# Audio tower on one core: second norm, routing and scatter of the first mixture moved into the recurrence, group by group

## What is computed

```python
h = tok(x, weight, bias)
h = h + lru(layernorm(h))              # complex diagonal recurrence over 166 steps, 256 states
h = h + moe16(layernorm(h))            # first mixture, below
h = h + sparse_attention(layernorm(h))
h = h + moe64(layernorm(h))            # dense over 64 experts, top 42
...
# first mixture
gate_logits = x @ gate_weight.T
top_vals, top_idx = jax.lax.top_k(gate_logits, TOP_K)     # 2 of 16
routing_w = jax.nn.softmax(top_vals, axis=-1)
h = jax.nn.silu(jnp.einsum('td,efd->tef', x, w1))
h_sum = jnp.einsum('tef,te->ef', h, mask)                  # per expert, over its tokens
h_mean = h_sum / jnp.maximum(counts, 1)[:, None]
y_mean = jnp.einsum('ef,edf->ed', h_mean, w2)
out = jnp.einsum('tk,tkd->td', routing_w, y_mean[top_idx])
```

## Time and profile before

| | us |
|---|---|
| median of 3 runs (2101.24 to 2106.53) | 2101.55 |
| span of the profiled execution | 2100.1 |
| profiled execution around its span, by the median | 1.45 |
| PE, DVE, ACT, POOL busy | 1869.5, 1683.1, 1385.2, 1349.0 |
| tokens, first norm, tables | 0 to 101.9 |
| recurrence, groups 0 to 3 | 101.9 to 188.4 |
| second norm and token product | 188.4 to 225.3 |
| routing on DVE | 225.3 to 252.4 |
| scatter by POOL (and late weights to 314.5) | 252.4 to 364.5 |
| 43 tiles, then the down product | 369.8 to 478.7 |
| attention, router of the second mixture | 478.7 to 884 |
| second mixture | 884 to 2100 |

### The profile page before, as it was taken

One profiled execution on the slowest core, in us unless ns is written; L12 is line 12 of the kernel. 1 busy time (PEld: TensorE's weight loads), 2 busy tenths in 40 slices (PEclk: granted clock), 3 DMA queues, 4 the chain that ended last, 5 costly groups with the idle time before them and its releaser, 6 DMA issues.

```text
span 2100.1 us, 50357 instructions
## 1 busy us (share of the span) xinstructions
PE 1869.5 (89%) x17138; PEld 1348.3 (64%) x17138; DVE 1683.1 (80%) x4788; ACT 1385.2 (66%) x2075; POOL 1349.0 (64%) x1027
## 2 busy tenths in 40 slices
PE   7889310888998997899999999999999999999998
PEld 5556200455657985677777777777777777777776
DVE  4775830865567859799999999999999999999998
ACT  4112350743444545688888888888888888888886
POOL 2100177007950003498998989899889989888887
PEclk9999655998998995699999999999999999999999
DMA  3613181622310020000000200000200000000000
GB/s 92 182 40 121 52 293 60 124 39 77 109 60 1 1 84 1 1 2 1 0 0 1 81 2 1 0 0 1 82 2 0 0 0 2 2 10 11 10 10 18
DMA packets 73500, 82.65 MB, mean 39 GB/s; under 512 B 38565, under 2 KB 56517, under 8 KB 71685
## 3 DMA queue, kind: packets, MB, share of 16 engines
q1 hardware_dynamic: 70660, 75.19, 12.0%
q0 software_dynamic: 2688, 5.44, 0.8%
HBM read 42.97 MB, written 29.20 MB: 34 GB/s over the span
## 4 chain that ended last, share of the span: by engine, by line
PE 58%; DVE 3%; issue 1%; ACT 1%; POOL 0%; ACTq 0%; DVEq 0%; POOLq 0%
PE bank L2447 29%; PE bank L2430 27%; DVE m_work L2321 1%; PE bank L405 1%; DVE m_best L2318 0%; DVE m_work L2312 0%; PE bank L414 0%; PE bank L2400 0%; DVE m_ut L851 0%; ACT m_h L2253 0%; DVE m_best L2311 0%; DVE m_ex L2323 0%; DVE h L2359 0%; POOL m_h L2198 0%; DVE m_red L2324 0%
## 5 line engine op out<-in xcount | busy, mean ns | idle before, releaser
L2447 PEld LDWEIGHTS bank<-weights,m_h 128*128 128x128 f16 x10752 | 639.3, 98 | 189.1 <-DVE hc L2350 95.2
L2198 POOL TENSOR_TENSOR m_h<-m_hidden,m_h 128x896 f16<-128x896 f32 x384 | 725.2, 1888 | 31.9
L2350 DVE SCALAR_TENSOR_TENSOR hc<-bank,m_shares,hc 128x128 f32<-128x128 f32 x2688 | 726.9, 341 | 4.0 <-PE bank L2447 4.0
L2447 PE MATMUL bank<-weights,m_h 128*128 128x128 f16 x10752 | 724.2, 219 | 2.3 <-POOL m_h L2198 2.3
L2250 ACT ACTIVATE m_hidden<-bank,m_b 128x896 f32<-128x896 f32 x384 | 386.7, 1007 | 183.1 <-PE bank L2430 183.1
L2335 DVE TENSOR_TENSOR m_h<-bank,m_h 128x896 f16<-128x896 f32 x384 | 419.0, 1091 | 101.8 <-ACT m_h L2253 101.8
L2196 POOL TENSOR_SCALAR m_h<-m_hidden 128x896 f16<-128x896 f32 x384 | 359.8, 937 | 104.2 <-ACT m_hidden L2250 78.9
L2430 PE MATMUL bank<-m_u_first,weights 128*128 128x448 f16 (+1 forms) x1536 | 417.9, 354 | 5.5 <-DVE h L2359 5.5
L2430 PE MATMUL bank<-m_u_second,weights 128*128 128x448 f16 (+1 forms) x1536 | 417.6, 354 | 0.0
L2247 ACT ACTIVATE bank<-bank,m_b 128x896 f32<-128x896 f32 x384 | 377.2, 982 | 0.7 <-PE bank L2430 0.7
L2253 ACT ACTIVATE m_h<-bank 128x896 f16<-128x896 f32 x384 | 348.7, 908 | 0.0
(11 more groups left out here) (333 smaller groups left out, 2165.6 us busy)
## 6 DMA issues: line engine op xcount, KB each, us to landing
weights<-expert_factors SPq DMA_DIRECT2D x12, 1024.0 KB, 7.8
expert_slots<-lru_zeros SPq DMA_DIRECT2D x1, 8256.0 KB, 32.0
lw_raw<-e_w_dram SPq DMA_DIRECT2D x16, 512.0 KB
expert_factors<-lw_made SPq DMA_DIRECT2D x16, 512.0 KB
ew_raw<-e_w_dram SPq DMA_DIRECT2D x16, 512.0 KB, 3.9
lru_wst<-w_dram SPq DMA_DIRECT2D x16, 256.0 KB, 2.7
weights<-w_dram SPq DMA_DIRECT2D x1, 4096.0 KB, 12.7
expert_factors<-ew_made SPq DMA_DIRECT2D x8, 512.0 KB, 3.1
```

What stands on the lines that cost most here:

```text
L2198: g.tensor_tensor(h1[:, x, 1], hidden[:, x], h1[:, x, 0], ALU.subtract).then_inc(second_of[1], 1)
L2350: last = v.scalar_tensor_tensor(acc[:, m * TW:(m + 1) * TW], y[q][:, (n - start) * TW:(n - start + 1) * TW], shares[:, m, e:e + 1], acc[:, ...
L2447: last = t.matmul(y[q][:, (n - start) * TW:(n - start + 1) * TW], factors[:, m, n * TW:(n + 1) * TW], k.weights[:, grp % 2, 2 + m, at], st ...
```

## The change

Routing becomes a class, `Routing`, whose parts are called from the recurrence's programs. A group has 11 tiles (`GT`), the last of 48 rows. While group g is in the recurrence, group g-1 is normed, routed and sent. Each expert has a fixed region of `REGION` rows in HBM, so a token's place is its expert's base plus a running count (`start`), and needs no totals of later groups. The rows behind an expert's last are zeroed at the end (`sync_fill`), and tiles are read at rows given by a register. The late weights move from ACT and DVE to POOL, behind the sends; SP stores them, and loads the down weights, between the tiles. The raw product lies where the down weights lay before (`k.weights[:, 1]`).

```diff
+REGION = -(-(T + ST) // ST) * ST
+SPARE = E0 * REGION
+GT = -(-GTOK // TW)
+PASSES = tuple((m, min(m + 3, GT)) for m in range(0, GT, 3))
@@ class Routing
+    def sync_fill(self, sp):
+        sp.wait_ge(self.tables, 1)
+        for e in range(E0):
+            row = sp.value_load(self.fill_i[0:1, e:e + 1], min_val=e * REGION, max_val=e * REGION + T)
+            sp.dma_start(k.slots[bass.ds(row, ST), :]..., blank).then_inc(self.filled, 16)
+    def pool_send(self, pool, r):
+        pool.wait_ge(self.second, r + 1)
+        pool.wait_ge(self.slots, r + 1)
+        for m in range(GT):
+            for q in range(2):
+                g.indirect_dma_start(out=self.k.slots, ...).then_inc(self.sent[r > 0], 16)
+    def pe_products(self, pe, r, b, y_added, u_ready):
+        if b == 0:
+            pe.wait_ge(y_added, STEP * (r + 1))
...
+        for m in range(first, end):
+            last = self.nc.tensor.matmul(out[0:rows_in(m), m - first], self.k.h[:, tokens_of(r, m)], self.cgi[:], ...)
+    def act_raw(self, act, r):
+            sc.activation(self.raw[:, first:end], self.token_bank(r, b), ACT.Copy).then_inc(self.raw_kept, 1)
...
+                last = sc.activation(self.u_tok[...], self.raw[:, m, 0:128], ACT.Square, accum_out=self.sums[:, m:m + 1])
+    def act_rows(self, act, r):
+        sc.activation(self.st[:, 1], self.st[:, 0], ACT.Sqrt).then_inc(self.root, 1)
...
+        for m in range(GT):
+            last = sc.activation(self.u_tok[...], self.raw[:, m, 0:128], ACT.Identity, scale=self.scale[:, m:m + 1])
+        act.wait_ge(self.gaps, r + 1)
+        sc.activation(self.gap[:], self.gap[:], ACT.Exp).then_inc(self.expd, 1)
@@ recurrence, POOL
+                if c == PERG + 1:
+                    routing.pool_start(pool)
+            for r in range(NGR):
+                routing.pool_send(pool, r)
@@ recurrence, ACT
-            for n in range(NC):
-                widen(n)
+            for g in range(NGR):
+                if g:
+                    routing.act_raw(act, g - 1)
+                    routing.act_rows(act, g - 1)
+                for i in range(STEP):
+                    widen(STEP * g + i)
@@ recurrence, DVE
                 if g + 1 < NGR:
                     state_part(g + 1, 0)
+                if g:
+                    routing.dve_scales(dve, g - 1)
+                    routing.dve_choose(dve, g - 1)
+                for i in range(2):
+                    add(g, i)
+                    split(STEP * g + i)
+                    if g == 0:
+                        normed(2 * PERG + 2 * i)
+                        normed(2 * PERG + 2 * i + 1)
+                if g:
+                    routing.dve_place(dve, g - 1)
+                    routing.dve_rows(dve, g - 1)
+                    routing.dve_weights(dve, g - 1)
                 if g + 1 < NGR:
                     state_part(g + 1, 1)
...
+            routing.dve_scales(dve, NGR - 1)
+            routing.dve_choose(dve, NGR - 1)
+            routing.dve_rows(dve, NGR - 1)
+            routing.dve_place(dve, NGR - 1)
+            routing.dve_weights(dve, NGR - 1)
+            routing.dve_tables(dve)
@@ recurrence, PE
+                if g:
+                    for b in range(len(PASSES)):
+                        routing.pe_products(pe, g - 1, b, y_added, u_ready)
                 for i in range(STEP):
+                    if i == 2 and g:
+                        routing.pe_rank(pe, g - 1)
                     output(g, i)
@@ first_mixture, SP
+            W2_AT = (2, 5, 8, 11)
+            KEEP_FROM, KEEP_EVERY = 4, 5
             for j in range(NST):
                 if j >= RING:
                     sp.wait_ge(up, PARTS * (j - RING + 1))
-                sp.dma_start_transpose(xt[:, j % RING], k.slots[j * ST:(j + 1) * ST, :])...
+                row = sp.value_load(row_i[0:1, j:j + 1], min_val=0, max_val=SPARE)
+                sp.dma_start_transpose(xt[:, j % RING], k.slots[bass.ds(row, ST), :])...
+                if j in W2_AT:
+                    sp.dma_start(w2[:, es], a["w2"][:, es]).then_inc(k.w2_in, 16)
+                if j >= KEEP_FROM and (j - KEEP_FROM) % KEEP_EVERY in (0, 2):
+                    late.sync_keep(sp)
@@ LateWeights
+    def sync_keep(self, sp):
+        self.sync_load(sp, i + 2)
+        sp.wait_ge(self.split, i + 1)
+        sp.dma_start(self.k.kept[...], self.made[:, i % 2]).then_inc(self.kept_out[i % 2], 16)
+    def pool_piece(self, pool, i):
+        g.tensor_copy(out[:, 0], raw).then_inc(self.rounded, 1)
+        g.tensor_tensor(left, raw, out[:, 0], ALU.subtract).then_inc(self.raw_read, 1)
+        g.tensor_scalar(left, left, 1.0 / SHARE, 1.0, ALU.mult, ALU.mult).then_inc(self.widened, 1)
+        g.tensor_tensor(out[:, 1], left, out[:, 0], ALU.add).then_inc(self.split, 1)
```

More of the change, by code:

```diff
@@ L531, in recurrence @@
+BIG = float(1 << 20)
+def recurrence(nc, k, tables, routing):
     a = k.a
@@ L552, in recurrence @@
         piece = E0 * FF0 // NC
-        wst = sb("wst", [128, 2, piece])
-        wide = sb("wide", [128, 2, piece])
-        zeros = sb("zeros", [128, 2 * 128], F16)
+        room = k.weights[:, 1].rearrange("p a b -> p (a b)")
+        raw_room, room = room[:, 8 * piece:], room[:, 0:8 * piece].bitcast(F32).rearrange("p (a b c) -> p a b c", a=2, b=2)
+        wst, wide = room[:, 0], room[:, 1]
+        routing.begin(ctx, on_diag[:], tables.work[:], va[:], raw_room)
         diag_ready = sem("diag_ready")
@@ L904, in first_mixture @@
         xt = sb("xt", [128, RING, 2, ST], F16)
[L906 to L911, removed]
+        rt = routing.rt
+        owner_i, row_i, owned = routing.owner_i, routing.row_i, routing.owned
         cleared = sem("outputs_cleared")
[L913 to L917, removed]
-        s = sem("routing_step")
-        expd = sem("exp_ready")
-        counted = sem("counted")
-        ranked = sem("ranked")
-        slots = sem("slots_ready")
-        shared = sem("weights_ready")
-        owners = sem("owners_ready")
-        turned = sem("weights_turned")
-        rt_ready = sem("rt_ready")
-        sent = sem("rows_sent")
         x_in = [sem(f"x_in{p}") for p in range(RING)]
@@ L1076, in _ @@
-            for q in range(2):
-                last = v.tensor_tensor_scan(halves(upto[:])[:, q], going[:].rearrange("p e n -> p (e n)"), totals[:, q], 0.0,
-                                            ALU.mult, ALU.add)
-            link(last)
-            count, whole, ends, start = few[:, 0], few[:, 1], few[:, 2], few[:, 3]
-            v.tensor_tensor(halves(place[:]), halves(upto[:]), totals, ALU.subtract)
-            link(v.tensor_scalar(whole, upto[:, :, NTW - 1], 1.0 / ST, 0.5 - 0.5 / ST, ALU.mult, ALU.add))
@@ L1099, in _ @@
-            link(v.reciprocal(tot[:, 1], tot[:, 0]))
-            v.tensor_tensor(wt[:], gap[:], wide(tot[:, 1]), ALU.mult).then_inc(shared, 1)
-            for i in range(late.count // 2):
-                late.dve_piece(dve, i)
-            link(v.tensor_tensor(past[:], line[:].unsqueeze(2).broadcast_to([128, NST, E0 - 1]),
-                                 ends[:, 0:E0 - 1].unsqueeze(1).broadcast_to([128, NST, E0 - 1]), ALU.is_ge))
-            link(v.tensor_reduce(owner[:], past[:], X, ALU.add))
@@ L1114, in _ @@
-            link(v.tensor_tensor(owned[:, 0], owned[:, 0], few[0:NST, 4], ALU.mult))
-            for i in range(late.count // 2, late.count):
-                late.dve_piece(dve, i)
             for j in range(PARTS * NST):
@@ L1191, in _ @@
                     pe.wait_ge(added, c - 3)
-                t.matmul(k.bank[:, c % 4, 0:CW], ym[:], k.hc[:, span(c)], start=True, stop=True).then_inc(out, 1)
+                t.matmul(k.bank[:, c % 4, 0:size(c)], ym[:], k.hc[:, span(c)], start=True, stop=True).then_inc(out, 1)
 class Choice:
```

640 lines of the change are left out of this document (387 added, 253 removed).

## The result

The changed kernel takes **2065.15 us** (median of 4 runs, 2062.78 to 2067.7), the kernel before 2101.39 beside it: a ratio of 0.9821, with a 95% interval of 0.9807 to 0.9835. The forecast was 2065. The total is right to the microsecond, and that is luck: the four executions alone lie 4.9 us apart, and errors of the working cancel. The experiments are mostly about that working. The profiled execution is the slowest of the four (2067.7); its span is 2065.9 us.

The account below looks back on a forecast made before the run. The path was taken as recurrence, second norm, routing, 112 us of POOL, then tiles. Sends gain 76 us, but slower tiles cut the gain to 37.0: 2100.1 - 37.0 = 2063.1 in the span, 2065 us as median; range 2044 to 2090.

Parts of the forecast that it names:

- Recurrence: Recurrence with norm and routing of each group inside it: ends at about 228 instead of 188.4, 40 us later.
- Sends: 88 sends on POOL beside the recurrence, 1.38 us each, POOL the bound from group 2: end at 288 instead of 364.5.
- the 3 us added for a slower TensorE: Added to the sends' end for TensorE running slower in groups 2 and 3 of the recurrence.
- The block change: Between the sends and the mixture's tiles: takes 1.0 us, so that POOL starts splitting pieces at 293.
- The tiles: First mixture: POOL's 6.6 us a piece holds the tiles, which leave 4.55; end at 410.9 instead of 447.9.
- 103 us of transfers: DMA work beside the tiles: transposes 45, pieces 47, down weights 11, in some 115 us; 4 us taken for it.
- Two signs: In the tiles' stretch: SP waiting for the splits, and POOL splitting without pause from about 293 to 400.
- Rival 1: Tiles are bound by DMA or SP, not POOL: loop ends 10 to 25 later, 2075 to 2090 us; chance 0.17.
- 91 us for SP: SP's need in the tile loop: 43 x (1.21 + 0.64) + 16 x 0.7, binding only if a register load exceeds 1.2.
- Rival 2: TensorE stays at its lower clock in the recurrence, slowing groups 2 and 3: 2073 to 2088 us; chance 0.12.
- Rival 3: Sends starve beside VectorE: before's end is reached at 1.96 us a send; at 2.4 the kernel takes 2140; chance 0.07.
- Rival 4: Tiles are not held back, as pieces run ahead: loop takes 78 us, kernel 2025 us; chance 0.08.

Follow-up runs that it names:

- pool_short_dma_light: Changed kernel with POOL splitting late pieces by two instructions, not four, and their loads and stores at an eighth of the bytes during the tiles: 2051.3 us, loop 105.4.

## Why the prediction was right, and where its steps were not

| step | forecast | measured |
|---|---|---|
| rows of groups 0, 1, 2 ready | 152.4, 188.3, 224.3 | 150.6, 185.9, 221.1 |
| a group's turn on VectorE | about 36 | 35.2 |
| last send ends | 288 | 277.9 |
| first piece on POOL | 293 | 290.4 |
| last split ends | 398.6, with DMA 402.6 | 402.6 |
| last tile sum | 410.9 | 411.4 |
| mixture's end (478.6 before) | not given | 443.0 |

**Recurrence: right, a little long.** Group 0's statistics were done at 134.9 instead of 136.6; from the scales to the rows it is 14.2 us against 14.3. Ahead of group 2's scales VectorE waited 7.22 us for the statistics; 7.5 was taken.

**Sends: right in kind, 10 us long.** Three terms: the rows came 3.2 us sooner; the 44 last sends took (277.93 - 221.38)/44 = 1.29 us each, not 1.38, worth 4.2; and the 3 us added for a slower TensorE were not needed. The first group, beside a busy VectorE, took (180.81 - 150.92)/22 = 1.36.

**The block change: the step that failed.** "A block change takes 1.0 us" was read from a block at whose end POOL had no sends to drain. The row for a block with sends stood in the same trace. The change puts a block's end directly behind the sends, so it pays 8.4 us, 7.4 more than taken.

**The tiles: right in length, wrong in cause.** The forecast compared two limits, POOL's 6.6 us a piece and the tiles' 4.55, and was right about these two; but the DMA engines, a third, were slower than both. From the first piece to the last split it took 112.2 us where 109.6 stood (16 x 6.6 and 4 for DMA). The runs show that halving POOL's work changes nothing and that bytes alone do. The forecast had worked out 103 us of transfers "in some 115" and then let them cost 4 us. Because the limits of POOL (112) and of the DMA engines (118) lie 6 us apart, the wrong one gave nearly the right time. Two signs named for it failed: SP waited only 2.4 us for the splits, and POOL, which was to split without pause, idled 7.4 us between pieces.

So the errors cancel, by luck: -10.1 on the sends, +7.5 to the first piece (5.0 forecast, 12.5 measured), +2.6 in the splitting, +0.5 from the last split to the last sum; together 0.5.

**Rivals.** Rival 1 named the right mechanism (DMA), and its 120 us for 103 us of transfers is the loop's 117.9 within 2 us (it used a share of 0.86; measured were 1.10 and 0.87). But the forecast's own loop, from 293 to 410.9, was already as long, so "10 to 25 later" did not follow. Its 91 us for SP was too short as well: its 16 issues of 0.7 leave out 14 loads of pieces and four of down weights, and 105 is what pool_short_dma_light shows. Rival 2: the mean granted clock fell to 0.90, 0.81, 0.84 and 0.70 between 134.9 and 248 (0.95 ahead of that), so TensorE had its lower level, 1.2 GHz, for part of the time. No cost of it shows on the path: the turns stayed at 35.2 us, VectorE waited 7.22 and 5.77 us for the statistics of groups 2 and 3, where 7.5 stood for group 2, and POOL's sends cover group 3. Rival 3: no send took over 1.59 us, and the mean of 1.29 to 1.36 with its gap lay far below the 1.96 from which it decides. The price that the Trainium skill ("SBUF — State Buffer", section "SBUF: two separate sides") gives for such a DMA beside a VectorE copy, 3100 ns, does not show in these 88 sends. It is not refuted either, since VectorE's plain copies beside them are a few casts of under 0.2 us. Rival 4, tiles that are not held: the loop is 117.9, not 78, and with all but two loads of the pieces out of the way it is still 88.5. So pieces do hold the tiles, but as traffic.

## What to carry to other kernels

When work is moved beside a loop, set up the limit of every resource it uses there (here 118, 112 and 105 us for DMA engines, POOL and SP), and take the largest. A time that comes out right doesn't show which one it was; the waits, and a run that changes one of them alone, do. When a queue of POOL's sends is moved to stand ahead of a block's end, look for the drain's row where that queue ended before. And what need not be finished in a loop that the DMA engines bind can be moved to a stretch behind it that moves nothing, as far as that stretch reaches: four of 16 pieces were worth 6 us there, and 14 made the kernel 39 us slower.

## What the runs showed of the hardware that was not expected

- POOL's drain holds a block's end about 7 us behind the last of a train of indirect DMAs (7.3 in the changed kernel, 6.9 before), though the sends had landed 2.3 us after their issue in the median and, in the changed kernel, the DMA engines were all but empty (share 0.01). Waiting for the landings instead took 1.3 us. What the drain does in that time, and whether it grows with the number of sends, was not tried.
- At a DMA share near 1, work taken off SP's queue came back as longer issues: with 30 issues less one transpose held SP for 6.9 us, and the loop moved by 1 us. With fewer bytes in flight the same transposes took SP 10.2 us less in all.
